# First attention's network: one activation per unit split into two of two banks, the next product entering half by half

## Chip, cores and metric

One core of one Trainium2 chip runs the whole kernel. The metric is the time on the device in microseconds (us), median of several executions. Durations of single instructions come from one profiled execution.

## What is computed

The reference is a decoder of two layers on x (4 sequences, 512 tokens, 256 features). Only the first attention of layer 0 is touched. Its scores of 16 heads go through a small network before the softmax:

```
combined = jnp.concatenate([attn_t, kerple_t], axis=-1)     # 16 scores and 16 distance terms
hdn = jax.nn.gelu(jnp.dot(combined, w1) + b1, approximate=False)   # 32 hidden
refined = jnp.dot(hdn, w2) + b2                             # 16
scores = scores + kerple[None] + refined
weights = jax.nn.softmax(where(causal, scores, -inf))
out = einsum('bhij,bhjd->bhid', weights, v)
```

This is done once for each of the 4 sequences (batches). The rest of the kernel (other attentions, the two feed-forward parts) is the same before and after.

## The kernel before

Queries are taken in four tiles of 128, the last first (`A_TI` = 3, 2, 1, 0). Tile i has L = 128 (i + 1) keys. A tile is cut into chunks: 4 each for i = 3, 2, 1 (chunks 0 to 3, 4 to 7, 8 to 11) and 2 for i = 0 (chunks 12, 13). A chunk is cut into units (`A_UNITS`): two units in each chunk of i = 3 and i = 2, one in each of the others, so 22 units per batch, 0 to 21; units 0 to 7 belong to i = 3, units 8 to 15 to i = 2. `FIRST[c]` and `LAST[c]` are the first and last unit of chunk c; for i = 3 and 2 the even unit is the first of its chunk and the odd one the last.

The network of unit k takes these steps:

- `up(k)` on TensorE (L1548 to L1561): 8 products with the scores (`fin`, L1553, start=True) and then the products with the distances (`kerA`, L1560, start=False) onto them. Each uses 32 rows and 64 columns of the array: group e (0 to 3) takes row group 32e and bank `A_UP + e`, and b (0, 1) the column half 64b. So eight different tiles of the array are used, one per (e, b). All four banks `A_UP` to `A_UP + 3` (0 to 3) are written, and `w1` is raised at the end. These banks exist once: `up(k)` waits for `gelu` to reach k, which is the activation of unit k - 1.
- the activation on ScalarE (L1672): one instruction reads 128 partitions x 4 banks x w columns (w = 512 for i = 3, 384 for i = 2), applies Gelu with a bias, and writes `hid` (named a_X in the rows), which is double-buffered.
- `down(k)` on TensorE (L1574): 8 products from `hid` to banks 4 and 5. Its release is `gelu` >= k + 1 and the sums of the unit before.
- `refined(k)` on VectorE: two additions onto `fin` (L1706), then the bias and row maximum (L1712).
- After the last unit of a chunk c, ScalarE runs `weights(c - 1)` (L1662): 4 exponentials of whole rows of the chunk before. Exp and Gelu need different activation tables, so a table load of 1.28 us stands ahead of the exponentials and another ahead of the next Gelu.
- VectorE divides (`normal`, L1725), TensorE transposes (`turn`, L1584) into banks 6 and 7, and VectorE copies them out (L1742). Products with the values (`weighted`, L1594) and the output product (L1600) use banks 6 and 7 too.

The order on TensorE is written out by hand: at step k comes `up(k + 1)`, then `down(k)`, then the transposes, value products and output products listed for that step. For k in `EXP_GAPS` (k = 4, 6, ..., the first unit of a chunk, as long as the tile has i >= 2) TensorE first waits until VectorE has added unit k - 1 (`mixed` >= 2k), and runs `keep_warm`, nine idle bf16 products (L407), before `up(k + 1)`. The waits for loads of `fin` (L1474 issues them on the SyncE queue) stand in `up` of the first unit of a chunk.

Of the kernel before, what the change touches and what calls it, by code (L numbers as in the profile page):

```python
# [18 lines left out]
ACT = mybir.ActivationFunctionType  # L19
AX = mybir.AxisListType  # L20

P = 128
# [196 lines left out]
def decoder(nc, io, out, rounds=B):  # L219
    ctx = ExitStack()  # L220
    with ctx:
        def sb(name, shape, dt=F32):
            return ctx.enter_context(nc.sbuf_tensor(name, shape, dt))
# [9 lines left out]
        x = sb("x", [P, NI, DM])  # L233
# [32 lines left out]
        kerA = sb("kerA", [P, NWIN])  # L266
        w1A = sb("w1A", [P, 2, 64])
        w2A = sb("w2A", [P, 32])
        b1A = sb("b1A", [P, 1])
# [4 lines left out]
        ps = ctx.enter_context(nc.psum_tensor("ps", [P, 8, BANK], F32))  # L274
# [1075 lines left out]
        AQ, AU = 16, 8  # L1350
# [6 lines left out]
        BACK = 504  # L1357
        A_UP, A_DOWN, A_TURN = 0, 4, 6
# [35 lines left out]
        def loaded(c):  # L1394

            return f"fin{c % 4 if c < SMALL else c}"

        def fin(c):

            if c < SMALL:  # L1400
                return M2["fin"][:, c % 4, :]
            half = (c - SMALL) % 2 * (CH_MAX // 2)
            return M2["fin"][:, (c - SMALL) // 2, half:half + CH_MAX // 2]

        def chunk(n):

            i, r = CHUNKS[n]
            return i, r, CH_R[i], (i + 1) * P


        A_UNITS = [(n, q) for n, (i, _) in enumerate(CHUNKS) for q in range(0, CH_R[i], 2 * SA_R[i])]
        NU = len(A_UNITS)
        FIRST = [min(k for k in range(NU) if A_UNITS[k][0] == n) for n in range(NCHUNK)] + [NU, NU + 1, NU + 2]
        LAST = [f - 1 for f in FIRST[1:NCHUNK + 1]]
        A_TURNS = [[(q, j) for q in range(0, CH_R[i], 4) for j in range(i + 1)] for i, _ in CHUNKS]
        ROWS_TO = [sum(CH_R[i] for i, _ in CHUNKS[:n]) for n in range(NCHUNK + 1)]
        TILE_END = {i: max(n for n in range(NCHUNK) if CHUNKS[n][0] == i) for i in range(NI)}

        V_HEADS = [4, 2, 1, 1]
        VALUES_AT = [[0, 0], [0, 0, 1, 1], [0, 0, 1, 1, 2, 2, 3, 3], [0, 1, 2, 3, 4, 4, 5, 5]]  # L1420

# [76 lines left out]
        def a_pe(pe, _, n, st):  # L1498
            g = lambda s: sm["A", s]
            m = M2  # L1500
# [38 lines left out]
            def up(k):  # L1539
                c, q0 = A_UNITS[k]  # L1540
                i, r, _, L = chunk(c)
                R = SA_R[i]
                if k == 1:
                    pe.wait_ge(g("fin_half"), 16)
                elif k == FIRST[c]:
                    pe.wait_ge(g(loaded(c)), 16 if c >= SMALL else 16 * (c // 4 + 1))
                if k:
                    pe.wait_ge(g("gelu"), k)  # L1548
                for e in range(4):
                    rows = slice(32 * e, 32 * e + 32)  # L1550
                    for b in range(2):
                        first = (q0 + b * R) * L
                        nc.tensor.matmul(ps[64 * b:64 * b + 64, A_UP + e, 0:R * L], w1A[rows, 0, :], fin(c)[rows, first:first + R * L],  # L1553
                                         start=True, stop=False, tile_position=(32 * e, 64 * b), skip_group_check=True)
                for q in range(R):
                    for e in range(4):
                        rows = slice(32 * e, 32 * e + 32)
                        for b in range(2):
                            t0 = BACK - i * P - AU * (r + q0 + b * R + q)
                            last = nc.tensor.matmul(ps[64 * b:64 * b + 64, A_UP + e, q * L:(q + 1) * L], w1A[rows, 1, :], kerA[rows, t0:t0 + L],  # L1560
                                                    start=False, stop=True, tile_position=(32 * e, 64 * b), skip_group_check=True)  # L1561
                last.then_inc(g("w1"), 1)

            def down(k):
                c, _ = A_UNITS[k]
                i, _, _, L = chunk(c)
                w = SA_R[i] * L
                pe.wait_ge(g("gelu"), k + 1)
                if k:
                    pe.wait_ge(g("mixed"), 2 * k)  # L1570
                for e in range(4):
                    for b in range(2):
                        rows = slice(64 * b, 64 * b + 64)
                        last = nc.tensor.matmul(ps[32 * e:32 * e + 32, A_DOWN + b, 0:w], w2A[rows, :], m["hid"][k % 2][rows, e, 0:w],  # L1574
                                                start=True, stop=True, tile_position=(64 * b, 32 * e))
                last.then_inc(g("w2"), 1)
# [11 lines left out]
            def weighted(y, i, v):  # L1588
                pe.wait_ge(g("bank_up"), BANK_OF["turn", TILE_END[i], len(A_TURNS[TILE_END[i]]) - 1] + 1)
                for t, j, e in itertools.product(range(V_HEADS[i]), range(i + 1), range(2)):  # L1590
                    h, r = 2 * (V_HEADS[i] * v + t) + e, AW * e
                    rhs = m["PT"][i, j].rearrange("p q (u h) -> p h q u", h=AH)[:, h]
# [20 lines left out]
            keep_warm(WARM_LOAD, bank=A_DOWN)  # L1613
            pe.wait_ge(g("s_up"), 4 * NI)
            up(0)
            pe.wait_ge(g("v_up"), 8)
            for k in range(NU + 4):
                if k in EXP_GAPS:
                    pe.wait_ge(g("mixed"), 2 * k)
                    keep_warm(WARM_EXP, bank=A_DOWN)  # L1620
                if k in DOWN_FIRST:
                    down(k)
                    up(k + 1)
                else:
                    if k + 1 < NU:
                        up(k + 1)
                    if k < NU:
                        down(k)
                for y in range(BANKS_TO[k], BANKS_TO[k + 1]):
                    if y >= 2:  # L1630
                        pe.wait_ge(g("bank_up"), y - 1)
                    what, a, b = A_BANKS[y]
                    if what == "turn":
                        turn(y, a, b)
                    elif what == "values":
                        weighted(y, a, b)
                    else:
                        out_product(y, a)

        def a_act(act, _, n, st):  # L1640
            g = lambda s: sm["A", s]
            m = M2
            for hq in range(NI):
                for k in range(NI):
                    i = A_TI[k]
                    L = (i + 1) * P
                    act.wait_ge(g("s_mm"), NI * hq + k + 1)
                    if hq:
                        act.wait_ge(g(f"out{i}"), 16 * 4 * hq)
                    nc.scalar.activation(m["Ss"][i].rearrange("p (h l) -> p h l", h=4), ps[:, 0:4, 0:L], ACT.Copy,  # L1650
                                         scale=AW ** -0.5).then_inc(g("s_up"), 1)
                    if hq >= 2:
                        e = NI * (hq - 2) + k
                        act.wait_ge(g("v_mm"), e + 1)
                        nc.scalar.activation(m["V"][:, e // 2, (e % 2) * BANK:(e % 2 + 1) * BANK], ps[:, 4 + e % 4, :], ACT.Copy).then_inc(g("v_up"), 1)

            def weights(c):
                _, _, R, L = chunk(c)
                act.wait_ge(g("negm"), c + 1)
                for q in range(R):  # L1660
                    row = fin(c)[:, q * L:(q + 1) * L]
                    nc.scalar.activation(row, row, ACT.Exp, bias=m["nm"][:, c % 4, q:q + 1],  # L1662
                                         accum_out=m["den"][:, c % 4, q:q + 1]).then_inc(g("exp"), 1)

            for k in range(NU):
                c, _ = A_UNITS[k]
                i, _, _, L = chunk(c)
                w = SA_R[i] * L
                act.wait_ge(g("w1"), k + 1)
                if k >= 2:  # L1670
                    act.wait_ge(g("w2"), k - 1)
                nc.scalar.activation(m["hid"][k % 2][:, :, 0:w], ps[:, A_UP:A_UP + 4, 0:w], ACT.Gelu, bias=b1A[:, 0:1]).then_inc(g("gelu"), 1)  # L1672
                if k == LAST[c] and c:
                    weights(c - 1)
            weights(NCHUNK - 1)

        def a_dve(dve, ch, n, st):
# [50 lines left out]
            for k in range(NU + 4):  # L1728
# [6 lines left out]
                for y in range(BANKS_TO[k], BANKS_TO[k + 1]):  # L1735
# [7 lines left out]
                    elif what == "values":  # L1743
                        nt = V_HEADS[a]
                        nc.vector.tensor_copy(m["OT"][:, nt * b:nt * b + nt, :], bank[:, 0:nt * P].rearrange("p (t q) -> p t q", t=nt)).then_inc(g("bank_up"), 1)
# [5 lines left out]
            dve.wait_ge(g("bank_up"), len(A_BANKS))  # L1751

        EXTRA["A"] = dict(pe=a_pe, act=a_act, dve=a_dve, pool=lambda *_: None, sp=a_sp)


# [349 lines left out]
```

## Time and profile before

| | us |
|---|---|
| median of 3 runs | 4195.28 (4194.73 to 4196.47) |
| the profiled execution | 4196.57 |
| its span, first to last instruction | 4194.8 |
| TensorE busy | 3778.7 (90% of the span) |
| VectorE busy | 2429.4 (58%) |
| ScalarE busy | 1740.9 (42%) |
| the stage of the network, batch 1 of 4 | about 126 to 275 |

The profile's first part gives the busy time of each engine over the whole span, so it averages stages that have different limits. The chain that ended last can be asked for a stretch alone, and then says what the stretch waited for, piece by piece. A timeline lists instructions merged by line: start, length, engine, line, shapes and, in brackets, how long the engine sat idle before and what ended that. PEld is the weight load of TensorE. An fp32 product leaves two weight loads and two matmul records, so the eight products of `up` with the scores stand as x16. The four batches repeat the stage at about 1162, 2199 and 3234 us.

### The profile page before, as it was taken

How to read it: one execution, taken by the hardware profiler on the slowest of the kernel's cores; microseconds unless marked ns; L12 is line 12 of the kernel's file. 1: busy time of each engine (PE TensorE's matmuls, PEld its weight loads, DVE VectorE, ACT ScalarE, POOL GpSimd, SP SyncE). 2: the span in 40 equal slices, each digit the busy share in tenths (PEclk: the TensorE clock that was granted, in tenths of full speed). 3: DMA queues.
4: the chain of work that ended last, by engine and by line, in shares of the span. 5: the costliest groups of instructions: out<-in, count | busy, mean ns of one | idle time of the engine just before them, and what ended most of it. 6: DMA issues, size and time to landing. Idle time of an engine off the chain costs nothing.

```text
span 4194.8 us, 58467 instructions
## 1 busy us (share of the span) xinstructions
PE 3778.7 (90%) x22074; PEld 1821.6 (43%) x22186; DVE 2429.4 (58%) x6089; ACT 1740.9 (42%) x3188; POOL 152.0 (4%) x168
## 2 busy tenths in 40 slices
PE   5898888999989987899998898899998989889999
PEld 2352444345435244435543524443553443444355
DVE  5568565732366856683237676667323766766642
ACT  1655433531274642362127374236113836423611
POOL 1000020000000001000000001000000000200000
PEclk9999989999999998899999999899999989989999
DMA  5313002122331201202242210120324120012031
GB/s 176 124 38 58 18 22 46 24 95 72 106 112 38 48 18 32 48 13 102 72 132 89 42 34 18 44 47 1 111 63 159 62 53 22 18 44 47 1 121 58
DMA packets 135286, 254.46 MB, mean 61 GB/s; under 512 B 23332, under 2 KB 82724, under 8 KB 130084
## 3 DMA queue, kind: packets, MB, share of 16 engines
q1 hardware_dynamic: 134984, 250.50, 21.2%
q8 instruction: 182, 2.98, 0.3%
q14 instruction: 120, 0.98, 0.1%
HBM read 156.04 MB, written 44.04 MB: 48 GB/s over the span
## 4 chain that ended last, share of the span: by engine, by line
PE 72%; DVE 14%; ACT 7%; SPq 4%; issue 3%; DMA 0%; DVEq 0%; POOLq 0%; ACTq 0%
PE ps L1223 11%; PE ps L584 7%; PE ps L567 6%; PE ps L1241 6%; PE ps L511 4%; DVE mx L748 4%; SPq L434 4%; PE ps L1594 3%; PE ps L407 3%; PE ps L1510 3%; PE ps L572 2%; ACT a_X L1672 2%; PE ps L463 2%; PE ps L1534 2%; DVE ps L745 2%
## 5 line engine op out<-in xcount | busy, mean ns | idle before, releaser
L683 ACT ACTIVATE PT<-ps 128x512 f32<-128x512 f32 (+2 forms) x1280 | 644.7, 564 | 351.3 <-PE ps L572 143.7
L748 DVE TENSOR_REDUCE mx<-ps 128x1 f32<-128x512 f32 (+3 forms) x768 | 432.4, 617 | 136.1 <-PE ps L514 80.3
L1223 PE MATMUL ps<-xnT,f_w 128*128 128x512 f32 x1088 | 490.0, 594 | 0.0
L567 PE MATMUL ps<-QS,KS 99*128 99x512 bf16 (+2 forms) x1280 | 432.5, 379 | 53.0 <-ACT PT L683 43.6
L511 PE MATMUL ps<-KS,QS 96*128 96x512 bf16 (+3 forms) x1280 | 428.1, 399 | 48.7 <-DVE mx L748 26.7
L745 DVE CUSTOM_DVE_ANT_0 ps<-ps,mneg 128x512 f32<-128x512 f32 x512 | 340.7, 717 | 88.7 <-PE ps L511 85.8
L584 PE MATMUL ps<-PT,VP 128*32 128x512 f32 (+3 forms) x2560 | 379.8, 581 | 0.0
L1329 DVE TENSOR_TENSOR f_tm<-f_si,ps 128x512 f32<-128x512 f32 x128 | 88.0, 687 | 491.8 <-ACT f_si L1281 491.6
L1281 ACT ACTIVATE f_si<-ps 128x512 f32<-128x512 f32 x136 | 80.8, 597 | 595.0 <-PE ps L1236 575.9
L567 PEld LDWEIGHTS ps<-QS,KS 99*128 99x128 bf16 x1280 | 110.5, 99 | 443.1 <-ACT PT L683 269.1
L1223 PEld LDWEIGHTS ps<-xnT,f_w 128*128 128x128 f32 x1088 | 206.6, 191 | 204.3 <-issue 197.8
L1241 PE MATMUL ps<-f_w,f_gu 128*128 128x256 f32 x1088 | 263.0, 385 | 9.5 <-DVE f_gu L1330 9.5
L511 PEld LDWEIGHTS ps<-KS,QS 96*128 96x128 bf16 x1280 | 132.5, 104 | 261.8 <-DVE mx L748 97.2
L1241 PEld LDWEIGHTS ps<-f_w,f_gu 128*128 128x128 f32 x1088 | 208.9, 193 | 82.9 <-issue 43.6
L1706 DVE TENSOR_TENSOR a_fin<-a_fin,ps 128x512 f32<-128x512 f32 (+1 forms) x176 | 104.5, 635 | 220.7 <-PE ps L1574 220.0
L1672 ACT ACTIVATE a_X<-ps,b1A 128x2048 f32<-128x2048 f32 (+1 forms) x88 | 159.6, 1814 | 128.4 <-PE ps L1560 127.8
L672 ACT ACTIVATE QS<-ps 3x512 bf16<-3x512 f32 x192 | 113.1, 589 | 229.7 <-PE ps L549 227.3
L407 PE MATMUL ps<-mneg,identb 128*128 128x512 bf16 x708 | 170.5, 389 | 39.6 <-DVE a_fin L1706 15.0
L572 PE MATMUL ps<-mnegT,identb 128*128 128x512 bf16 x460 | 178.2, 387 | 0.0
L1510 PE MATMUL ps<-wbuf,a_Y 128*128 128x512 f32 x256 | 128.8, 647 | 24.1 <-issue 22.7
L1662 ACT ACTIVATE a_fin<-a_fin,a_nm 128x512 f32<-128x512 f32 (+3 forms) x256 | 140.5, 550 | 7.7 <-DVE a_nm L1716 7.1
L768 DVE RECIPROCAL rq<-ps 128x16 f32<-128x16 f32 x48 | 12.4, 258 | 224.8 <-PE ps L521 224.8
(275 smaller groups left out, 5482.9 us busy)
## 6 DMA issues: line engine op xcount, KB each, us to landing
f_w<-in_wF SPq DMA_DIRECT2D x136, 384.0 KB, 3.1
scores<-a_fin SPq DMA_DIRECT2D x64, 256.0 KB, 3.0
a_fin<-scores SPq DMA_DIRECT2D x32, 512.0 KB, 4.6
a_Y<-in_wA SPq DMA_DIRECT2D x5, 3072.0 KB, 15.2
KS<-KP SPq DMA_DIRECT2D x240, 64.0 KB, 2.3
scores<-a_fin SPq DMA_DIRECT2D x64, 192.0 KB, 3.1
a_fin<-scores SPq DMA_DIRECT2D x12, 1024.0 KB, 7.9
a_fin<-scores SPq DMA_DIRECT2D x16, 768.0 KB, 4.4
```

Source lines behind the costliest of these rows:

```text
L407: nc.tensor.matmul(ps[:, bank, :], identb[:, :], mneg[:, 0, 0:BANK], start=True, stop=True)
L511: last = nc.tensor.matmul(o, m["QS"][0:KR, h, i * P:(i + 1) * P], m["KS"][0:KR, h, f:f + w], start=True, stop=not c.causal)
L567: last = nc.tensor.matmul(o, m["KS"][0:KST, h, j * P:(j + 1) * P], m["QS"][0:KST, h, q0:S], start=True, stop=plain)
L572: last = nc.tensor.matmul(o, identb[:, :], mnegT[:, j, :], start=False, stop=True)
L584: last = nc.tensor.matmul(ps[r:r + 32, 6, q0:S], m["VP"][:, j, h, :], m["PT"][:, mp % 2, j % 2, e, 0:S - q0], start=(j == 0), stop=(j == c ...
L683: nc.scalar.activation(m["PT"][:, mp % 2, j % 2, e, 0:w], ps[:, SLOTS + n % TURNED, 0:w], ACT.Exp, scale=HD ** -0.5).then_inc(g("exp"), 1)
L745: nc.vector.tensor_tensor_reduce(ps[:, k % SLOTS, 0:w], ps[:, k % SLOTS, 0:w], mneg[:, i, f:f + w], 1.0, NEG, ALU.add, ALU.max, m["mx"][:, ...
L748: nc.vector.tensor_reduce(m["mx"][:, h % 2, i, f // BANK:f // BANK + 1], ps[:, k % SLOTS, 0:w], AX.X, ALU.max, negate=True).then_inc(g("sl ...
L1223: last = nc.tensor.matmul(ps[:, 2 * v + e % 2, :], m["w"][:, e % NRING, (2 * v + k) * P:(2 * v + k + 1) * P], xnT[:, k, :], start=(k == 0) ...
L1241: last = nc.tensor.matmul(ps[:, 6 + i // 2, (i % 2) * DM:(i % 2 + 1) * DM], m["gu"][:, e % 2, i * P:(i + 1) * P], m["w"][:, e % NRING, 2 * ...
L1510: last = nc.tensor.matmul(ps[:, 4 + e % 4, :], m["w"][:, k, col:col + P], xnTA[:, k, :], start=(k == 0), stop=(k == KD - 1))
L1672: nc.scalar.activation(m["hid"][k % 2][:, :, 0:w], ps[:, A_UP:A_UP + 4, 0:w], ACT.Gelu, bias=b1A[:, 0:1]).then_inc(g("gelu"), 1)
```

## The change

`HALVES[k]` is 2 for units of chunks that have two units (i = 3 and 2, units 0 to 15) and 1 for the others; `HIDDEN_TO` counts the activations. ScalarE issues two activations for a unit with two halves, each over two banks, each with its own wait on `w1` and its own increment of `gelu`. On TensorE, `up` of the first unit of a chunk keeps its order and raises `w1` by `HALVES[k]` at its end. `up` of the second unit of a chunk is reordered: the four score products of banks 0 and 1 after the first half of the activation before; then, after its second half, the four score products of banks 2 and 3 alternating with the four distance products of banks 0 and 1, and one increment; then the four distance products of banks 2 and 3, and one increment.

```diff
+        HALVES = [2 if FIRST[c] != LAST[c] else 1 for c, _ in A_UNITS]
+        HIDDEN_TO = [sum(HALVES[:k]) for k in range(NU + 1)]
...
-                if k:
-                    pe.wait_ge(g("gelu"), k)
-                for e in range(4):
+                def scored(e, b):
...
+                def distant(e, b, q):
...
+                tiles = list(itertools.product(range(4), range(2)))
+                if k == FIRST[c]:
+                    if k:
+                        pe.wait_ge(g("gelu"), HIDDEN_TO[k])
+                    for e, b in tiles:
+                        scored(e, b)
+                    for q in range(R):
+                        for e, b in tiles:
+                            last = distant(e, b, q)
+                    last.then_inc(g("w1"), HALVES[k])
+                else:
+                    pe.wait_ge(g("gelu"), HIDDEN_TO[k] - 1)
+                    for e, b in tiles[:4]:
+                        scored(e, b)
+                    pe.wait_ge(g("gelu"), HIDDEN_TO[k])
+                    for (e, b), (e2, b2) in zip(tiles[:4], tiles[4:]):
+                        scored(e2, b2)
+                        last = distant(e, b, 0)
+                    last.then_inc(g("w1"), 1)
+                    for e, b in tiles[4:]:
+                        last = distant(e, b, 0)
+                    last.then_inc(g("w1"), 1)
...
-                pe.wait_ge(g("gelu"), k + 1)
+                pe.wait_ge(g("gelu"), HIDDEN_TO[k + 1])
...
-                act.wait_ge(g("w1"), k + 1)
                 if k >= 2:
                     act.wait_ge(g("w2"), k - 1)
-                nc.scalar.activation(m["hid"][k % 2][:, :, 0:w], ps[:, A_UP:A_UP + 4, 0:w], ACT.Gelu, bias=b1A[:, 0:1]).then_inc(g("gelu"), 1)
+                n = 4 // HALVES[k]
+                for x in range(HALVES[k]):
+                    act.wait_ge(g("w1"), HIDDEN_TO[k] + x + 1)
+                    nc.scalar.activation(m["hid"][k % 2][:, n * x:n * x + n, 0:w], ps[:, A_UP + n * x:A_UP + n * x + n, 0:w], ACT.Gelu,
+                                         bias=b1A[:, 0:1]).then_inc(g("gelu"), 1)
```

`scored` and `distant` issue the same products, with the same operands, as the loops that they replace.

## Rows read from the trace of the kernel before

**Rows 1.** The page: busy time of the engines over the span.

```profile
PE 3778.7 (90%) x22074; PEld 1821.6 (43%) x22186; DVE 2429.4 (58%) x6089; ACT 1740.9 (42%) x3188; POOL 152.0 (4%) x168
```

**Rows 2.** The chain that ended last, from 124 to 222 us, shares by line.

```profile
by line: ACT a_X L1672 24.0%; PE ps L1553 14.2%; PE ps L1560 11.5%; ACT a_fin L1662 10.5%; PE ps L1594 7.8%; ACT L1662 6.5%; ACT L1672 6.5%; PE ps L407 6.3%; issue 5.2%; PE ps L1574 4.3%; PE ps L1584 3.4%
```

**Rows 3.** The same chain in pieces (start, length), units 4 to 6 (i = 3).

```profile
149.89 1.98 ACT a_X L1672
...
151.92 1.12 PE ps L1553 x16
...
154.00 1.97 ACT a_X L1672
...
155.99 1.28 ACT L1662
...
161.53 1.98 ACT a_X L1672
```

**Rows 4.** The same chain, units 8 and 9 (i = 2).

```profile
173.16 1.55 ACT a_X L1672
...
174.75 0.91 PE ps L1553 x16
...
176.41 1.54 ACT a_X L1672
```

**Rows 5.** The same chain from unit 12 on.

```profile
193.43 1.55 ACT a_X L1672
...
195.02 0.91 PE ps L1553 x16
...
196.57 0.81 PE ps L1574 x16
...
205.19 1.89 PE ps L407 x8
207.08 0.83 PE ps L1553 x16
```

**Rows 6.** Timeline of narrow windows: records of `up(2)` (PE), weight loads of `down(1)` (PEld).

```profile
136.20 0.69 PE L1553 MATMUL ps<-a_fin,w1A 32*64 32x512 f32 x8 [1.17 <-ACT a_X L1672]
...
137.51 0.67 PE L1560 MATMUL ps<-kerA,w1A 32*64 32x512 f32 x8
...
138.10 0.18 PEld L1574 LDWEIGHTS ps<-a_X,w2A 64*32 64x32 f32 x16 [0.81 <-issue]
```

**Rows 7.** Groups by line and shape: the activation of a unit.

```profile
L1672 ACT ACTIVATE a_X<-ps,b1A 128x2048 f32<-128x2048 f32 x56 | 110.3, 1969 | 92.7 <-PE ps L1560 92.3
...
L1672 ACT ACTIVATE a_X<-ps,b1A 128x1536 f32<-128x1536 f32 x32 | 49.4, 1543 | 35.7 <-PE ps L1560 35.5
```

**Rows 8.** Timeline of ScalarE: two activations with a bias, back to back.

```profile
1736.86 0.69 ACT L645 ACTIVATE KP<-ps,bkE 128x512 bf16<-128x512 f32 x1 [0.45 <-PE ps L463]
1737.44 0.68 ACT L649 ACTIVATE val<-ps,bkE 128x512 f32<-128x512 f32 x1
```

**Rows 9.** Timeline around the `keep_warm` of steps 6 and 8.

```profile
159.22 1.28 DVE L1706 TENSOR_TENSOR a_fin<-a_fin,ps 128x512 f32<-128x512 f32 x2 [0.49 <-PE ps L1574]
...
160.78 1.89 PE L407 MATMUL ps<-mneg,identb 128*128 128x512 bf16 x8 [0.65 <-DVE a_fin L1706]
...
170.42 1.28 DVE L1706 TENSOR_TENSOR a_fin<-a_fin,ps 128x512 f32<-128x512 f32 x2
...
171.99 1.89 PE L407 MATMUL ps<-mneg,identb 128*128 128x512 bf16 x8 [0.65 <-DVE a_fin L1706]
```

**Rows 10.** Timeline of TensorE: `up(1)` in batches 1, 2 and 3.

```profile
130.34 1.99 PE L1553 MATMUL ps<-a_fin,w1A 32*64 32x512 f32 x16 [2.22 <-ACT a_X L1672]
...
1167.77 1.73 PE L1560 MATMUL ps<-kerA,w1A 32*64 32x512 f32 x16
...
2205.05 1.10 PE L1560 MATMUL ps<-kerA,w1A 32*64 32x512 f32 x16
```

**Rows 11.** The page: loads of a chunk of i = 2, size and time to landing.

```profile
a_fin<-scores SPq DMA_DIRECT2D x16, 768.0 KB, 4.4
```

More of the change, by code:

```diff
@@ L1546, in up @@
                     pe.wait_ge(g(loaded(c)), 16 if c >= SMALL else 16 * (c // 4 + 1))
-                if k:
-                    pe.wait_ge(g("gelu"), k)
-                for e in range(4):
+                def scored(e, b):
                     rows = slice(32 * e, 32 * e + 32)
[L1551 to L1561, printed above, removed]
@@ L1562, in up @@
-                last.then_inc(g("w1"), 1)
+                    first = (q0 + b * R) * L
+                    nc.tensor.matmul(ps[64 * b:64 * b + 64, A_UP + e, 0:R * L], w1A[rows, 0, :], fin(c)[rows, first:first + R * L],
+                                     start=True, stop=False, tile_position=(32 * e, 64 * b), skip_group_check=True)
+                def distant(e, b, q):
+                    rows = slice(32 * e, 32 * e + 32)
+                    t0 = BACK - i * P - AU * (r + q0 + b * R + q)
+                    return nc.tensor.matmul(ps[64 * b:64 * b + 64, A_UP + e, q * L:(q + 1) * L], w1A[rows, 1, :], kerA[rows, t0:t0 + L],
+                                            start=False, stop=True, tile_position=(32 * e, 64 * b), skip_group_check=True)
```

## The prediction

> **What bounds the kernel now.** I read the page first. TensorE is busy for nine tenths of the span, ScalarE for four tenths [rows 1]. That is an average and says little about this stage, so I asked for the chain that ended last between 124 and 222 us, the first 16 units of batch 1. There the Gelu activation is the largest entry with 24.0%, the two halves of the upward product (L1553, L1560) follow with 25.7% together, and exponentials and table loads with 23.5% [rows 2]. The reader is to see that activation and product alternate: neither engine is full, each waits for the other, because the four banks exist once.
>
> In pieces, for i = 3: Gelu of unit 4 starts at 149.89, the product of unit 5 at 151.92, its Gelu at 154.00, and at 155.99 it is over [rows 3]. So from the first start to the second end are 6.10 us: 1.97 + 0.06, 2.08 of product, 1.99. For i = 2 the same reads 173.16, 174.75, 176.41 [rows 4]: the product part is 1.66 us. Then follow table load, four exponentials and table load, until 161.53, where the next chunk's first Gelu starts [rows 3]. Under those exponentials the product of the next chunk's first unit is hidden, so only the second unit of each chunk has its product exposed. From 195.02 on, after the Gelu of unit 12, the chain stays on TensorE: product, `down`, value products, `keep_warm`, and `up(15)` at 207.08 directly behind `keep_warm` of 205.19 + 1.89 [rows 5]. Units 13 to 21 are therefore no longer held by ScalarE.
>
> **The change, part by part.** (a) *The product enters half by half.* A product's record leaves in rounds: eight records start together at 136.20 and the fourth round at 137.51 [rows 6], so a round is 0.44 us and one fp32 product, two rounds, 0.87 us at 512 columns; at 384 columns three quarters, 0.65. Before, 4 rounds and a tail (2.08 - 4 x 0.44 = 0.32) stood between two Gelus. Now the score products of banks 0 and 1 (two rounds) run beside the second half of the activation: half of 2048 columns takes 1.11 us by the slope below, more than 0.87. After that half, two rounds carry the rest of the scores beside the first distances, the first half of the next Gelu starts, and the last two rounds run beside it (0.87 against 1.0 until the second half wants them). So 4 exposed rounds become 2: minus 0.87 us per pair in i = 3, minus 0.65 in i = 2.
>
> (b) *One activation becomes two.* 2048 elements take 1969 ns and 1536 take 1543 [rows 7]: 426 ns per 512, and 1969 - 4 x 426 = 265 ns fixed. Two activations back to back overlap: a row of 0.69 us is followed after 0.58 [rows 8], so by 0.11. A split costs 0.265 - 0.11 = 0.16 us. From below the bound is 0 (a longer overlap), from above 0.265 (none, since the second half has its own wait); I take 0.16, as these rows too are activations with a bias reading a bank. The Trainium skill (ScalarE: Activation LUTs, section What ACT_TABLE_LOAD costs) gives about 280 ns fixed with a bias operand and an overlap of about 93 ns, an estimate of 0.19 a split; by the page my sum would give back 0.03 x 13 x 4 = 1.6 us more. The row's shorter duration decides here.
>
> Net of two splits, a pair gains 0.87 - 0.32 = 0.55 in i = 3 (4 pairs: units 0-1 to 6-7) and 0.65 - 0.32 = 0.33 in i = 2 (pairs 8-9 and 10-11). The Gelu of unit 12 is split before the chain leaves ScalarE: +0.16. Units 13, 14 and 15 gain nothing, TensorE is the bound there, and their splits lie under it. If that cover were gone they would cost 0.48.
>
> (c) *What is late next: `keep_warm`.* It waits for VectorE's sum of the unit before, and `up` stands behind it. In chunk 3 VectorE adds at 170.42 with no idle time ahead, so this addition doesn't come earlier; it comes 0.16 later with the split of unit 6. `keep_warm` ends at 171.99 + 1.89 + 0.16 = 174.04 [rows 9]. The first half of the Gelu of unit 8 now ends at 173.16 + 0.90 - 0.55 = 173.51 [rows 4, 7]. The 0.65 of score products then end at 174.69, the second half of the Gelu at 173.51 + 0.80 = 174.31: 0.35 late. At step 6 there were 0.49 us of idle time ahead of the addition [rows 9]; there I get 0.1. In the later chunks it is in time. Sum +0.45; bounds 0 and 0.9.
>
> (d) *Waits and increments.* TensorE gets one more wait per second unit. Behind the wait for the second half stand the mixed products, then `down`, which needs that half anyway. The unsplit product of a first unit waits for both halves as before. Cost nothing: covered by the same event. `down` starts as long after the end of the Gelu as before. No transfer is added or moved; loads of 4.4 us stand in chunk periods of 10 to 11.6 us which shrink by half a microsecond [rows 3, 11].
>
> (e) *The clock.* In batch 1 `up(1)` comes after 2.22 us of idle TensorE, and its first product takes 1.99 instead of 1.12 us: the granted clock is at the lower of its levels, 1.2 instead of 2.4 GHz. In batch 2 the second product takes 1.73 instead of 1.10, in batch 3 nothing is lost [rows 10]; batch 4 is like 2. Together 1.7 + 0.6 + 0.6 = 2.9 us. The change shortens that idle time to about 1.3 us. Bounds: 2.9 gained, or 1 lost if it falls at a worse place. I take 1.0 gained, nearer to batch 3, which shows that the drop isn't due each time.
>
> **Sum.** Per batch 4 x 0.55 + 2 x 0.33 - 0.16 - 0.45 = 2.25; times 4 batches is 9.0; with the clock 10.0 us. The profiled execution took 4196.57 and would take 4186.6; it lay 1.3 us above the median, so from the median 4195.3 I get 4185.3 us, 0.24% less. About 0.2%, 8.4 us, is what a measurement of this kernel can tell from no change.
>
> **Rivals.** *The array blocks (B).* In `up(15)` TensorE isn't waiting for ScalarE: scores of banks 2 and 3 and distances of banks 0 and 1 come at once, and the first distance product stands behind its own tile's two rounds. If what is behind it can't pass, the other tiles idle for 0.65 us per batch: 2.6 in all, 4187.9. For it: no row shows a tile passing another that is busy. Against it: nothing either, since all groups of before visit the eight tiles evenly. It can't touch the pairs on ScalarE's chain, as their tiles are free by then.
>
> *No overlap (C).* The second activation, with a wait of its own, starts only after the first has ended: 0.11 more for 13 splits in 4 batches, 5.7 us, and 4191.0. Against it: the second activation of [rows 8] has a wait of its own as well.
>
> *Not in effect (D).* The first half's signal doesn't let TensorE in earlier. Then 13 x 0.16 x 4 = 8.3 are lost, the clock gains nothing, and the time is 4203.6. No row speaks for it; the waits on `gelu` end 0.05 us after the activation now [rows 3].
>
> *Slower: the mixed group doesn't run side by side (E).* It alternates products that start a sum with products that add to one, in two sets of banks. If the array takes two more rounds for it, every pair gives 0.87 (0.65) back: per batch 6 pairs at -0.32, -0.16 and -0.65 for unit 15, 2.7 lost, 11 us in all: 4206. It decides from 0.55 us more per pair, little over one round. Against it: the sixteen weight loads of eight products lie within 0.18 us, and eight records start as one [rows 6], though a product's two rounds need each other's end; tiles already run independently, whichever line they are of. The Trainium skill (TensorE: Matmul & The Clock Gate, section Part 3: Packing small matmuls) states that matmuls start and end strictly in program order; this would speak for B and E.
>
> **Chances.** Forecast 0.50; B 0.22; C 0.15; D 0.03; E 0.05; 0.05 for the clock or something unnamed in either direction. Within the forecast, the split at 0.07 instead of 0.16 and the full 2.9 of the clock would give 4179, `keep_warm` at 0.9 and no clock gain 4188. The range 4181.5 to 4192.0 takes in most of that, B, and most of C. Faster by over 0.2% means below 4186.9: four fifths of the forecast, two fifths of B, 0.50 in all; slower D and E, 0.07; same the rest, 0.43.
>
> **What the profile would show.** The half Gelu at 1.11 us (0.90 for i = 2), the second starting 1.0 after the first; in the chain of batch 1, from the first Gelu of chunk 2 to the end of its last 5.5 us instead of 6.10; between the end of a second half and the next unit's first half 1.2 us instead of 2.1; `up(9)` starting behind `keep_warm`; chunk periods of 11.1 instead of 11.6. B shows as `up(15)` 0.65 longer; E as mixed records starting one after another. I would be wrong if the distance from the second half's end to the next Gelu stays at 2 us, or if the stage shortens by 2 us per batch but the rest of the kernel grows.

## The result and the profile after

The changed kernel takes 4186.16 us in the median of 13 runs (4182.52 to 4189.42); the kernel before takes 4195.28 in the median of 13 on the same chip (4191.47 to 4201.22). The ratio is 0.9977, with a 95% interval of 0.9968 to 0.9985: 0.23% less, and between 0.15% and 0.32% by the interval. So it is faster, but whether by more than the 0.2% of the forecast stays a near thing. 4185.3 was predicted. The profiled span went from 4194.8 to 4184.4.

The page's busy line, to be read against [rows 1]:

```profile
PE 3809.9 (91%) x22186; PEld 1825.0 (44%) x22186; DVE 2431.0 (58%) x6089; ACT 1751.2 (42%) x3252; POOL 152.0 (4%) x168
```

ScalarE has 64 instructions more (one for each of 16 split units in 4 batches) and 10.3 us more work, 0.16 for each. TensorE does the same products; its matmul records are 112 more because the earlier profile lacks some, so its busy time tells nothing here.

The chain that ended last, 124 to 222 us, shares by line (the view cuts this line off itself), against [rows 2]:

```profile
by line: PE ps L1554 21.8%; PE ps L407 15.2%; PE ps L1560 11.2%; PE ps L1616 11.1%; PE ps L1596 10.5%; ACT a_X L1696 9.3%; DVE a_fin L1731 6.2%; PE ps L1606 5.6%; ACT a_fin L1684 2.5%; issue 1.6%; ACT L1684 1.3%; ACT L1696 1.3%; DVE a_fin L
```

Gelu fell from 24.0% to 9.3% of the chain, and `keep_warm` (L407) rose from 6.3% to 15.2%. That looks like a new bound, and it is nearly a tie. ScalarE's timeline shows how little hangs on it (against [rows 3, 4]; x2 is a unit's two halves):

```profile
147.43 2.12 ACT L1696 ACTIVATE a_X<-ps,b1A 128x1024 f32<-128x1024 f32 x2
150.89 2.12 ACT L1696 ACTIVATE a_X<-ps,b1A 128x1024 f32<-128x1024 f32 x2 [1.33 <-PE ps L1560]
...
158.56 2.12 ACT L1696 ACTIVATE a_X<-ps,b1A 128x1024 f32<-128x1024 f32 x2
162.16 2.12 ACT L1696 ACTIVATE a_X<-ps,b1A 128x1024 f32<-128x1024 f32 x2 [1.47 <-PE ps L1560]
...
169.84 1.69 ACT L1696 ACTIVATE a_X<-ps,b1A 128x768 f32<-128x768 f32 x2
172.65 1.69 ACT L1696 ACTIVATE a_X<-ps,b1A 128x768 f32<-128x768 f32 x2 [1.12 <-PE ps L1560]
```

Units 4 to 9 stand here. From one unit's start to the next it was 4.11, 7.53, 4.10, 7.53, 3.25 before; now it is 3.46, 7.67, 3.60, 7.68, 2.81. So each second unit of a chunk starts 0.65, 0.50 and 0.44 us sooner behind the first, and each first unit of a chunk 0.14 or 0.15 later behind the second. Chunk periods of i = 3 fell from 11.63 to 11.13 and 11.28, the idle time between two Gelus from 2.13 to 1.33.

From unit 12 on the chain lies on TensorE as it did in [rows 5], and `up(15)` starts directly behind `keep_warm`:

```profile
201.37 1.94 PE ps L407 x9
203.32 0.85 PE ps L1554 x16
```

**Where the time went.** A good ruler is the stage's length, from the first record of `up(0)` to the first record of `up(21)`. In batch 3 these are 2199.98 and 2327.57 before, 2193.77 and 2319.06 after. For every kernel of this study, in us:

| | batch 1 | 2 | 3 | 4 | sum |
|---|---|---|---|---|---|
| before | 129.28 | 128.17 | 127.58 | 128.24 | 513.27 |
| after | 125.41 | 125.26 | 125.29 | 125.32 | 501.28 |
| e1, split only | 130.65 | 130.71 | 130.64 | 130.53 | 522.53 |
| e2, late entry | 130.59 | 130.60 | 130.86 | 130.56 | 522.61 |
| e3, not alternating | 125.23 | 125.28 | 125.31 | 125.25 | 501.07 |
| e4, before + idle products at step 0 | 127.67 | 127.65 | 127.69 | 127.65 | 510.66 |
| e5, whole from unit 12 | 125.25 | 125.16 | 125.20 | 125.26 | 500.87 |
| e6, short `keep_warm` | 126.49 | 126.66 | 126.77 | 126.76 | 506.68 |
| e7, no `keep_warm` at 14, 16 | 122.53 | 122.44 | 122.45 | 122.44 | 489.86 |
| e8, order of waits | 124.96 | 125.20 | 124.92 | 125.17 | 500.25 |
| e9, e5 + e7 + e8 | 121.03 | 120.89 | 121.07 | 121.04 | 484.03 |

In batch 3 the kernel before loses no clock at `up(1)` [rows 10]. Against four times 127.58, its batches 1, 2 and 4 are 1.70, 0.59 and 0.66 longer, 2.95 in sum. Of this, 1.68, 0.59 and 0.53 stand between `up(1)` and `up(2)`, where the clock fell: 2.80. The other 0.15 come further back, where batches of one kernel differ by about 0.1 anyway. None of the 2.80 is left after. The rest, 4 x 127.58 - 501.28 = 9.04, is the restructured stage. So the stages gave 11.99 us and the span 10.4: outside them the execution is 1.6 us longer. The windows from `up(21)` of batch 4 to the end, before and then after (length, busy times, granted clock as a share, DMA):

```profile
3362.76:4194.80 832.04, 757.51 (x3663) 368.80 (x3675) 481.27 (x1211) 309.60 (x632) 33.46 (x37) 0.95 0.18 46
```

```profile
3349.56:4184.40 834.84, 762.60 (x3683) 370.45 (x3675) 481.61 (x1211) 311.16 (x637) 33.43 (x37) 0.95 0.18 46
```

This part, which the change doesn't touch, is 2.8 us longer; another such part, between the stages of batches 3 and 4, is 1.8 shorter (906.95 and 905.18). They vary so between the other profiles too (832.9 to 835.8 for the first; all that lies outside the four stages takes 3677.9 to 3687.5 in the eleven profiles). I put it down to where the clock falls in them, which wasn't tested. From here on a statement about the stage rests on the table; the whole time has this scatter on top.

### The profile page after: what moved, and what is told of

Read it like the earlier page. It is cut to its first block, busy times and chain, and to the rows that moved or that the text cites. A ratio compares the mean times of both kernels' runs of the same rounds, so it can differ in the third digit from the quotient of the medians.

```text
span 4184.4 us, 58643 instructions
## 1 busy us (share of the span) xinstructions
PE 3809.9 (91%) x22186; PEld 1825.0 (44%) x22186; DVE 2431.0 (58%) x6089; ACT 1751.2 (42%) x3252; POOL 152.0 (4%) x168
## 4 chain that ended last, share of the span: by engine, by line
PE 75%; DVE 14%; SPq 4%; ACT 4%; issue 2%; DMA 0%; DVEq 0%; POOLq 0%; ACTq 0%
PE ps L1223 11%; PE ps L584 7%; PE ps L567 6%; PE ps L1241 6%; PE ps L407 4%; SPq L434 4%; PE ps L511 4%; DVE mx L748 4%; PE ps L1616 3%; PE ps L1513 3%; PE ps L572 3%; PE ps L1554 2%; PE ps L463 2%; PE ps L1537 2%; DVE ps L745 2%
## 5 line engine op out<-in xcount | busy, mean ns | idle before, releaser
L407 PE MATMUL ps<-mneg,identb 128*128 128x512 bf16 x768 | 184.8, 390 | 28.6 <-DVE a_fin L1731 10.9
L1696 ACT ACTIVATE a_X<-ps,b1A 128x1024 f32<-128x1024 f32 (+2 forms) x152 | 169.3, 1157 | 72.0 <-PE ps L1560 71.4
L572 PE MATMUL ps<-mnegT,identb 128*128 128x512 bf16 x512 | 198.0, 387 | 0.0
L1672 ACT ACTIVATE a_fin<-ps 128x2048 f32<-128x2048 f32 (+1 forms) x64 | 79.2, 1237 | 152.4 <-PE ps L1537 151.7
```

The costliest lines, as they stand in the source:

```text
L407: nc.tensor.matmul(ps[:, bank, :], identb[:, :], mneg[:, 0, 0:BANK], start=True, stop=True)
L572: last = nc.tensor.matmul(o, identb[:, :], mnegT[:, j, :], start=False, stop=True)
L1696: nc.scalar.activation(m["hid"][k % 2][:, n * x:n * x + n, 0:w], ps[:, A_UP + n * x:A_UP + n * x + n, 0:w], ACT.Gelu, bias=b1A[:, 0:1]).th ...
```

## The experiments

**e1: only the split.** Every `up` keeps the old order and waits for both halves.

```diff
-                if k == FIRST[c]:
+                if True:
...
-                else:
...
```

> The activations of units 0 to 15 stay in two halves, but the upward product of a chunk's second unit has its old order again and waits for both halves. Only the price of the split is left. My theory: 0.16 us for each of the 13 splits on ScalarE's chain (units 0 to 12) in 4 batches, 8.1 us more than before, about 4203.4; two half activations of 512 columns a bank end 2.12 us after their start, chunk periods of i = 3 are 11.9 instead of 11.6, and the drops of the clock at the stage's first gap are back. Rival C (no overlap): 0.265 each, 13.8 us more. Rival 'the split is free': 0, about 4195.3, and then the gain of the change came from elsewhere.

4207.56 in the median of 7 runs, ratio 1.0025 (1.0013 to 1.0036). The stages are 9.26 longer than before for 13 x 4 splits: 0.18 each. The chain that ended last, batch 1 (L1684 is the activation here):

```profile
137.97 2.13 ACT a_X L1684 x2
...
140.14 1.12 PE ps L1554 x16
141.25 0.94 PE ps L1560 x16
...
142.27 2.12 ACT a_X L1684 x2
```

Gelu to Gelu is 4.30 where [rows 3] have 4.11. So the split by itself is a loss, of about the forecast size. The early entry is worth 522.53 - 501.28 = 21.25 us. Some 2.8 of that are clock: without the entry TensorE idles 2.37 us ahead of `up(1)`, and from the Gelu of unit 0 to that of unit 1 it is 5.03, 5.12, 5.05 and 4.88 us in the four batches, where an estimate without a drop is 4.33 (4.18 in batch 3 before, and 0.15 for the split).

**e2: the new order without the early entry.** The one wait for the second half stands ahead of all products.

```diff
-                    pe.wait_ge(g("gelu"), HIDDEN_TO[k] - 1)
+                    pe.wait_ge(g("gelu"), HIDDEN_TO[k])
                     for e, b in tiles[:4]:
                         scored(e, b)
-                    pe.wait_ge(g("gelu"), HIDDEN_TO[k])
```

> As the changed kernel (halves, mixed order, two increments), but the first four score products wait for the second half of the activation as well. My theory: what gains is the entry of these four beside the second half; without it four rounds stand again before the next first half, so 2.1 us instead of 1.27 from the end of a second half to the next first half, and the time is that of the split alone, 4203. Rival 'the early increment of w1 alone gives part of it': 1.7 us and a time about half way, 4194. Rival B (the array blocks behind a distance product whose tile is busy): each of the 8 second units takes one product's time longer until the second half, 0.87 or 0.65 us, and the chunks lose more, above 4210.

4207.3 in the median of 8, ratio 1.0029 (1.0019 to 1.004), and stages as in e1 (522.61 and 522.53). The chain, batch 1:

```profile
140.68 1.14 PE ps L1554 x16
141.82 0.99 PE ps L1560 x16
142.81 2.11 ACT a_X L1695 x2
```

The product takes its four rounds again. The second signal on `w1` brings nothing by itself: the eight tiles work side by side, so banks 0 and 1 are ready only 0.05 us ahead of banks 2 and 3 (142.62 and 142.68 in this `up(3)`). The gain is all from the two rounds that run under the activation's second half.

**e3: scores and distances not alternating.** First the four score products, then the four distance products.

```diff
-                    for (e, b), (e2, b2) in zip(tiles[:4], tiles[4:]):
-                        scored(e2, b2)
+                    for e, b in tiles[4:]:
+                        scored(e, b)
+                    for e, b in tiles[:4]:
                         last = distant(e, b, 0)
```

> As the changed kernel, but after the second half the four score products of banks 2 and 3 come first and then the four distance products of banks 0 and 1, instead of alternating. My theory: tiles run independently, so the order in the program of products on different tiles costs at most their issue, some 0.03 us a pair: 1.27 to 1.30 us from the end of a second half to the next first half, stage as short as with the change. Rival 'strict order': the alternation matters, and the distance would grow by a round or more (0.43).

A single execution: 4186.09, span 4184.4, stages 501.07 (after: 501.28). Its chain in batch 3, units 2 and 3:

```profile
2202.76 1.12 ACT a_X L1697
...
2206.21 2.13 ACT a_X L1697 x2
```

The distance is 3.45; the changed kernel has 3.46 there (2203.63 and 2207.09). So where `up` enters in time the order among products of different tiles doesn't matter. In `up(7)`, which enters late behind `keep_warm`, it does a little: from the Gelu of unit 6 to that of unit 7 it is 3.52 here and 3.60 after, in all four batches. So alternating costs about 0.07 us per batch.

**e4: the kernel before with five idle products ahead of `up(1)`.** The clock by itself.

```diff
                     keep_warm(WARM_EXP, bank=A_DOWN)
+                if k == 0:
+                    keep_warm(5, bank=A_DOWN)
```

> The kernel before, with five idle bf16 products (about 1.2 us) behind up(0), where TensorE waits 2.22 us for the first activation of a batch. Nothing on the chain is removed. My theory: this idle time is why the granted clock fell at up(1) in three of four batches; with it cut to 1.0 us the clock stays, up(1) takes 2.07 in all batches, and 2.8 us are gained in a profile like that of before, 4192.5. Rival 'chance': the clock falls as often as before, no gain, 4195.3.

4191.91 in the median of 10, ratio 0.9989 (0.9979 to 0.9998). All four stages take 127.65 to 127.69. The chain in batch 1 (L1674 is the activation here):

```profile
129.83 1.98 ACT a_X L1674
...
131.94 1.12 PE ps L1553 x16
133.06 0.93 PE ps L1560 x16
```

The scores of `up(1)` took 1.99 us in [rows 10]; here they take 1.12. Counted from the start of its stage, `up(2)` comes 1.68, 0.59, 0.00 and 0.53 us sooner in the four batches: all 2.80 that were lost there. In batch 3, where there was nothing to win, the starts stay equal to `up(14)`, so the idle products cost nothing; the 0.11 by which that stage is longer come from `up(15)` and later. So the clock was lost to that idle time, and the changed kernel, which shortens it, wins the same.

**e5: units 12 to 15 whole.** Activation and product as before in chunks 6 and 7.

```diff
-        HALVES = [2 if FIRST[c] != LAST[c] else 1 for c, _ in A_UNITS]
+        HALVES = [2 if FIRST[c] != LAST[c] and c < 6 else 1 for c, _ in A_UNITS]
...
-                if k == FIRST[c]:
+                if k == FIRST[c] or HALVES[k] == 1:
```

> As the changed kernel, but units 12 to 15 have one activation and the old order. My theory: their splits and halves gain nothing, because TensorE is the bound from up(13) on; the split of unit 12 is saved, so up(14) and everything behind it in the stage comes 0.16 us earlier per batch, 0.6 us in all, too little for the time to show. Rival: the early entry of up(13) and up(15) does help, and the stage is longer by up to 0.65 per batch without it.

A single execution: 4184.74. At `up(14)` every batch is 0.16 to 0.18 us ahead of after, the split of unit 12; at `up(21)` 0.06 to 0.16. The new order of `up(13)` and `up(15)` is worth nothing and costs nothing.

**e6: five idle products instead of nine at steps 4 to 12.** The lateness of `keep_warm` by itself.

```diff
-                    keep_warm(WARM_EXP, bank=A_DOWN)
+                    keep_warm(5 if k < 14 else WARM_EXP, bank=A_DOWN)
```

> As the changed kernel, with five instead of nine idle products at steps 4 to 12. My theory: keep_warm has become late at steps 6 and 8, at a price of about 0.4 us per batch together; five products end 0.9 us sooner, so up(7) and up(9) start with the first half of the activation, the distance from second half to next first half is 1.27 in all pairs, and the stage is 0.4 us shorter per batch than with the change, 1.5 us in all, if the clock holds. Rival: keep_warm isn't what delays, and the activations of units 6 and 8 keep their shifts. Second rival: the clock falls somewhere for lack of these products, and the stage is longer.

A single execution: 4195.9. The `keep_warm` of steps 4, 6 and 8 of batch 1 now end 0.4 to 0.9 us ahead of `up`, and the distance from unit 6 to unit 7 is 3.46 (160.10 to 163.56) instead of 3.60, from 8 to 9 it is 2.82 instead of 2.81: the lateness was 0.15 at step 6 and nothing at step 8. But the stages are 5.40 us longer, for another reason. Timeline of TensorE, batch 2, step 4 (of the five idle products four are on record):

```profile
1181.41 1.03 PE L407 MATMUL ps<-mneg,identb 128*128 128x512 bf16 x4 [1.68 <-DVE a_fin L1731]
1183.31 2.16 PE L1554 MATMUL ps<-a_fin,w1A 32*64 32x512 f32 x12 [0.88 <-ACT a_X L1696]
```

and the window of that product:

```profile
1183.30:1186.70 3.40, 3.39 (x28) 1.35 (x32) 1.04 (x3) 0.96 (x1) 0.00 (x0) 0.52 0.00 0
```

The granted clock is 0.52 there, the lower level, and `up(5)` loses 1.2 to 1.5 us in every batch; after's window at the same place has 1.00. The nine idle products are paid back here by the clock, and the second rival of the expectation came true.

**e7: no `keep_warm` at steps 14 and 16.** There the chain lies on TensorE and the idle products are on it [rows 5].

```diff
-        EXP_GAPS = [LAST[c] + 1 for c in range(1, SMALL)]
+        EXP_GAPS = [LAST[c] + 1 for c in range(1, SMALL) if LAST[c] + 1 < 14]
```

> As the changed kernel, without the idle products at steps 14 and 16, where the chain lies on TensorE. My theory: there each of them is 2.1 us of pure path, and TensorE is busy all the time anyway, so the clock needs no help: about 4 us less per batch, 16 in all, unless ScalarE becomes the bound at units 15 to 17 and keeps a part; 4186 - 16 = 4170, at worst 4178. Rival: the wait for the addition that stands with keep_warm is then paid in down instead, and nothing is gained, 4186.

4178.63 in the median of 5, ratio 0.9959 (0.9945 to 0.9973); 2.8 to 2.9 us less per batch, not the 4 that the two rows of about 2 us promise: from `up(14)` to `up(15)` some 1.9 are won, from `up(16)` to `up(17)` only 0.9. The chain of batch 1 says why:

```profile
209.36 0.95 PE ps L1560 x32
...
210.33 0.02 ACTq L1695
...
210.38 1.28 ACT L1696
...
211.67 1.98 ACT a_X L1696
...
213.69 1.09 PE ps L1596 x16
```

`down(16)` waits 3.3 us for a table load and the activation of unit 16: ScalarE is late next. The table load starts only after `up(16)` has ended, though its engine had nothing to do from 209.35 on. That is the same cause as in e8.

**e8: the order of two waits.** In the diff, ScalarE's wait on `w1` came to stand behind the wait on `w2`. Here it stands first again.

```diff
-                if k >= 2:
-                    act.wait_ge(g("w2"), k - 1)
...
                     act.wait_ge(g("w1"), HIDDEN_TO[k] + x + 1)
+                    if k >= 2 and x == 0:
+                        act.wait_ge(g("w2"), k - 1)
```

> As the changed kernel, but ahead of a unit's first half the wait for w1 stands before the wait for w2, as in the kernel before. My theory from the trace of the change: of two waits the second in the program becomes an instruction of its own on ScalarE's sequencer; with w1 second it is that instruction which waits for the product, and the activation starts 0.16 us after the product's end where it was 0.09. With w1 first the 0.07 are back for units 2, 3, 5, 7, 9 and 11, so the stage is 0.4 us shorter per batch, 1.6 in all, 4184.5. Rival: the order of waits costs nothing, the 0.07 belong to the split itself, and the starts don't move.

4183.29 in the median of 10, ratio 0.9974 (0.9965 to 0.9984); by this the whole time can't be told from after's. The chain can. After, batch 3, unit 2:

```profile
2203.55 0.02 issue
2203.57 0.02 ACTq L1695
2203.59 0.04 issue
2203.63 1.12 ACT a_X L1696
```

and e8 at the same place:

```profile
2201.10 0.93 PE ps L1560 x16
2202.03 0.02 issue
2202.05 1.12 ACT a_X L1696
```

From the product's end to the activation's start it is 0.08 after and 0.02 in e8; units 0 and 1, which have no second wait, show 0.02 after as well. `ACTq` is an instruction of ScalarE's queue that does nothing but wait. There is one for a unit with two waits, and it holds the later one of the program. With `w2` there it is over early; with `w1` there it ends last, and its successor's start comes on top, 0.06 to 0.07 us. The stages are 1.03 us shorter in sum, and at `up(14)` each batch is 0.3 ahead.

The table load ahead of unit 16 shows the larger side of it. After, it waits; in e8 it has run before the product ends (ScalarE's timelines, batch 1):

```profile
211.48 1.28 ACT L1696 ACT_TABLE_LOAD   x1 [1.03 <-PE ps L1560]
```

```profile
210.80 1.28 ACT L1696 ACT_TABLE_LOAD   x1
```

**e9: e5, e7 and e8 together.** To see whether they add up, and as a version that could beat both.

> The changed kernel with three things together: w1 waited for before w2, units 12 to 15 whole and in the old order, no idle products at steps 14 and 16. My theory: the single gains add, 0.4 and 0.15 to the 2.8 us per batch that the missing idle products gave; the stage ends 14 to 15 us a batch-sum earlier than before plus the 2.8 of the clock; 4178.6 - 2.2 = 4176.4. Rival: ScalarE is the bound at units 14 to 16 there, and the parts overlap, 4178.6.

4168.49 in the median of 5, ratio 0.9941 (0.9927 to 0.9954), 25 us less than before and 8 less than expected. The stages are 17.25 shorter than after, where e5, e7 and e8 alone give 0.41 + 11.42 + 1.03 = 12.86. With the other 4.4 counted to e7, that experiment comes to 15.8, the 4 per batch that its rows promised. They are what unit 16 took away there: its table load now runs early (208.54 to 209.82; `up(16)` ends at 209.57), and the chain of batch 1 doesn't touch ScalarE any more behind unit 12. That it is the order of waits and not e5's part shows in the time from the Gelu of unit 15 to that of unit 16 (batch 1): 7.83 after, 7.83 in e7 and 7.80 in e5, but 6.83 in e8 and 6.67 in e9.

```profile
209.57 1.96 PE ps L1616 x16
211.53 0.59 PE ps L1606 x4
212.12 1.02 PE ps L1596 x16
```

## Why the prediction was right, and where its steps were off

The forecast case came true: 9.0 us were worked out for the stage and 9.04 measured (9.4 against e4's stages, which lose no clock either), and the total is 0.9 us beside the predicted one. The mechanism is the predicted one, but that the numbers meet so closely is luck: several terms were off and cancelled.

**(a) The early entry** held. Its terms were 0.87 less 0.16 for a split, so 0.71 per second unit of i = 3, and 0.49 for i = 2. Measured are 0.65 (units 4 to 5) and 0.44 (units 8 to 9), both short by 0.05 to 0.06, which is the wait of (d): in e8 they are 0.71 and 0.50. The first pair, units 0 and 1, gained 0.79 (4.18 to 3.39), 0.08 more than forecast: `up` enters there 0.14 us after the activation and not 0.04, and this delay now lies under the second half as well. e1 and e2 show that all of it hangs on the entry.

**(b) The split** held. Groups by shape, against [rows 7]:

```profile
L1696 ACT ACTIVATE a_X<-ps,b1A 128x1024 f32<-128x1024 f32 x64 | 67.8, 1111 | 43.2 <-PE ps L1560 43.1
...
L1696 ACT ACTIVATE a_X<-ps,b1A 128x768 f32<-128x768 f32 x64 | 54.2, 898 | 28.5 <-PE ps L1560 28.3
```

Two halves of 1.11 take 2.12 together (2.22 less an overlap of 0.10), the whole took 1.97: 0.15 for a split, forecast 0.16. e1's 0.18 has the wait of (d) in it. The estimate of 0.19 from the Trainium skill (ScalarE: Activation LUTs, section What ACT_TABLE_LOAD costs) was a little high. With this rival C falls: the second half starts 1.01 us after the first though it has a wait of its own.

**(c) The late `keep_warm`** was mis-sized: forecast 0.1 + 0.35, measured 0.15 + 0. The place was right, the size was not (and 174.69 - 174.31 is 0.38, not the 0.35 that the prediction wrote). Timeline of TensorE around steps 6 and 8, against [rows 9]:

```profile
157.99 2.12 PE L407 MATMUL ps<-mneg,identb 128*128 128x512 bf16 x9 [0.43 <-DVE a_fin L1731]
160.03 1.38 PE L1554 MATMUL ps<-a_fin,w1A 32*64 32x512 f32 x12
...
168.79 2.12 PE L407 MATMUL ps<-mneg,identb 128*128 128x512 bf16 x9 [0.53 <-DVE a_fin L1731]
170.84 1.28 PE L1554 MATMUL ps<-a_fin,w1A 32*64 32x384 f32 x9
```

At step 8 `keep_warm` ended 0.72 us after its unit's Gelu had started [rows 9, 4]; now it ends at 168.79 + 2.12 = 170.91 against 169.84, so 1.07 after. It lost 0.35; I had it lose 0.55 + 0.16 = 0.71, as if VectorE's work stood still while the Gelu moved ahead by a pair's gain. But that work hangs on the sum of unit 6, which came earlier with its Gelu. The lateness left is 0.06 at the entry of `up(9)`, and the mixed products wait for the second half of the Gelu anyway. e6 confirms both sizes.

**(d) "Waits and increments cost nothing"** was wrong, and is the one step that failed in kind. I looked at TensorE's new wait and not at the order of ScalarE's two. Some 0.06 per exposed unit (2, 3, 5, 9 and 11), 0.3 per batch, shown by e8; at unit 7, which the expectation of e8 had counted too, nothing comes back, since `keep_warm` is late there (3.60 and 3.59). And table loads go behind the wait: the Gelus of units 16, 17 and 18 start 1.45 us after their product's end, where before it was 0.11 to 0.27. This costs nothing here, where the chain lies on TensorE, and at unit 16 about 1.1 us per batch, 4.4 in all, as soon as `keep_warm` is gone. The 0.3 nearly equals what (c) overpriced, so the sum came out right for a reason that I hadn't seen.

**(e) The clock** gave nearly its upper bound of 2.9, 2.80 at `up(1)`, where I took 1.0. Timeline of TensorE, `up(1)` of batch 1, and the windows of before in batches 1 and 3 and of after in batch 1 there (the number behind the five busy times is the granted clock):

```profile
129.78 1.55 PE L1554 MATMUL ps<-a_fin,w1A 32*64 32x512 f32 x9 [1.37 <-ACT a_X L1696]
```

```profile
130.30:134.00 3.70, 3.66 (x40) 1.15 (x45) 0.00 (x0) 0.00 (x0) 0.00 (x0) 0.54 0.69 258
2203.80:2207.60 3.80, 3.00 (x48) 0.87 (x48) 0.25 (x1) 1.58 (x2) 0.00 (x0) 1.00 0.81 312
```

```profile
129.70:132.00 2.30, 2.22 (x28) 0.83 (x32) 0.00 (x0) 1.03 (x2) 0.00 (x0) 1.00 1.09 446
```

After 2.22 us of idle time the clock falls in batches 1, 2 and 4 and not in batch 3; after 1.37 it stays full in all four. With 2.37 (e1) it falls in all four. The row of batch 3, nearest to which I chose, showed a drop that sometimes doesn't come; it said nothing about a shorter idle time. The 1.8 us too little here and the 1.6 us that the rest of the kernel gained in length, which was no term of mine, cancel too.

**Rivals B and E** fall. In `up(7)` the program has a score product of a free tile, then a distance product of a busy one, alternating. The weight loads come in that order, within 0.06 us from 160.74 on. The matmuls don't (timeline of TensorE, batch 1):

```profile
160.03 1.38 PE L1554 MATMUL ps<-a_fin,w1A 32*64 32x512 f32 x12
160.94 0.61 PE L1560 MATMUL ps<-kerA,w1A 32*64 32x512 f32 x4
161.22 0.63 PE L1554 MATMUL ps<-a_fin,w1A 32*64 32x512 f32 x4
161.37 0.91 PE L1560 MATMUL ps<-kerA,w1A 32*64 32x512 f32 x8
```

Twelve score records start before the first distance record: eight of banks 0 and 1, and the first rounds of all four products of banks 2 and 3, the last of these five places behind the distance product that starts at 160.94. So products of free tiles pass one whose tile is busy, and both kinds run side by side. What is left of B is the 0.07 us per batch that e3 shows in this place. `up(15)`, where B had its price, takes 1.49 us from its first record at 203.25 to `down` at 204.74; before it was 1.48, from 207.01 to 208.49. The Trainium skill's statement (TensorE: Matmul & The Clock Gate, section Part 3: Packing small matmuls) that matmuls start and end strictly in program order doesn't hold for the starts on different tiles here. **Rival D** is what e2 shows, 4207.3, and after isn't it.

What stays open: why the untouched rest of the kernel took 1.6 us more in this profile, and whether the clock falls in it are the cause.

## What to carry to other kernels

Splitting an activation pays only where the next product really enters after its first half: here each pair of units pays two splits of 0.15 us and hides 0.87 us of product. When a block is rewritten, keep the wait that ends last first in the program, above all where a table load would go behind it. Idle products that hold the clock are worth their time where the engine would stand idle anyway, and cut short there they lose more than they save (5.4 us in e6); on the path of the engine itself they are pure cost (nearly 4 us per batch in e9).

## What the runs showed of the hardware that was not expected

- Of two waits ahead of an activation, the second in the program becomes a waiting instruction of its own in ScalarE's queue: 0.02 us for itself and 0.04 to the activation, when it is the one that ends last. The table load ahead of the activation then waits as well (211.48 against 210.80 for its start; from product to activation 1.45 us against 0.38 at unit 16).
- A matmul on a free tile starts ahead of an earlier one in the program whose tile is busy, by 0.16 to 0.19 us in `up(7)`, though the weight loads of both are in order.
- The granted clock fell to the lower level after 2.22 us of idle TensorE in three of four batches, after 2.37 in four of four (e1), and after 1.37 in none; five instead of nine idle products in a gap were too few to hold it (e6), five were enough at `up(1)` (e4).
